# Delta rule: the next batch's key projections placed around the inverse's first levels

## The reference, cut to what matters

```python
q = _causal_dw_conv_silu(x @ Wq, conv_q)   # k and v likewise
q = _l2norm(q)
k = _l2norm(k)
def step(state, inp):
    q_t, k_t, v_t, a_t, b_t = inp
    retained = jnp.einsum('bhvk,bhk->bhv', state, k_t)
    rk = retained[..., None] * k_t[:, :, None, :]
    vk = v_t[..., None] * k_t[:, :, None, :]
    state = a4 * (state - b4 * rk) + b4 * vk
    o_t = jnp.einsum('bhvk,bhk->bhv', state, q_t)
    return (state, o_t)
```

## Time and profile before

| | us |
|---|---|
| median of 3 runs | 3834.85 |
| lowest and highest | 3829.89, 3841.63 |
| the profiled execution: its time | 3837.73 |
| its span | 3836.0 |
| PE busy | 3293.1 (86%) |
| DVE busy | 2394.9 (62%) |
| delta stage, first projection to last product | 1711.7 to about 3312 |

### The profile page before, as it was taken

The page is one execution under the profiler, slowest core; times in us unless marked ns, Lnnn a source line. Parts: engine busy times, 40 slices in busy tenths (PEclk is TensorE's granted clock), DMA queues, the critical chain, the costliest instruction groups (busy, mean ns, idle before and its releaser), DMA issues. The chain is left out here.

```text
span 3836.0 us, 48336 instructions
## 1 busy us (share of the span) xinstructions
PE 3293.1 (86%) x17898; PEld 2559.0 (67%) x17898; DVE 2394.9 (62%) x5793; ACT 1272.0 (33%) x2457; POOL 171.1 (4%) x165
## 2 busy tenths in 40 slices
PE   5999938889999999647989898989898989588887
PEld 2665524445999999625777777777777779455554
DVE  6788425544777777757676767575757574354542
ACT  2333202222444444314343434342434332023332
POOL 0000000024101111000000000000000000000000
PEclk8999958999999999867778787777768685588786
DMA  1000080022898899740101010101010100100000
GB/s 62 22 17 11 12 159 12 11 82 96 313 323 317 320 320 317 247 143 28 39 29 39 29 40 28 39 29 39 29 39 29 37 18 1 58 12 20 14 17 11
DMA packets 203644, 326.78 MB, mean 85 GB/s; under 512 B 37449, under 2 KB 157522, under 8 KB 202258
## 3 DMA queue, kind: packets, MB, share of 16 engines
q1 hardware_dynamic: 196930, 305.94, 24.1%
q0 software_dynamic: 6480, 17.77, 1.2%
HBM read 275.15 MB, written 48.50 MB: 84 GB/s over the span
## 5 line engine op out<-in xcount | busy, mean ns | idle before, releaser
L767 PE MATMUL ex_ps<-ex_xbT,ex_w 128*128 128x128 f32 x4544 | 530.6, 275 | 0.6 <-issue 0.5
L767 PEld LDWEIGHTS ex_ps<-ex_xbT,ex_w 128*128 128x128 f32 x4544 | 524.1, 192 | 4.7 <-issue 0.7
L1376 PE MATMUL de_ps<-de_hT,de_w 128*128 128x512 f32 x640 | 312.0, 642 | 19.2 <-DMA de_w<-in_w_kqv_dram 13.8
L896 ACT ACTIVATE ex_t<-ex_ps,ex_b 128x128 f32<-128x128 f32 x568 | 208.5, 367 | 335.3 <-PE ex_ps L767 303.5
L711 PE MATMUL ex_ps<-ex_xT,ex_w 128*128 128x512 f32 x512 | 230.4, 607 | 12.5 <-DVE ex_gl L1008 9.1
L1376 PEld LDWEIGHTS de_ps<-de_hT,de_w 128*128 128x128 f32 x640 | 128.5, 208 | 167.5 <-issue 158.9
L1008 DVE SCALAR_TENSOR_TENSOR ex_gl<-ex_ps,ex_b,ex_t 128x128 f32<-128x128 f32 (+1 forms) x316 | 123.5, 391 | 137.1 <-ACT ex_t L896 69.8
L711 PEld LDWEIGHTS ex_ps<-ex_xT,ex_w 128*128 128x128 f32 x512 | 97.9, 194 | 132.0 <-issue 115.2
L1748 DVE SCALAR_TENSOR_TENSOR de_ya<-de_kx,de_taps,de_ya 128x512 f32<-128x512 f32 x192 | 141.9, 750 | 50.7 <-ACT de_ya L1596 46.1
L1492 PE MATMUL de_ps<-de_vb,de_DG 128*128 128x64 f32 x512 | 113.2, 422 | 56.9 <-DVE de_o L1921 47.6
L1008 DVE SCALAR_TENSOR_TENSOR ex_gm<-ex_ps,ex_b,ex_t 128x128 f32<-128x128 f32 (+1 forms) x316 | 121.7, 385 | 47.7 <-ACT ex_t L869 41.9
(11 more groups left out here) (377 smaller groups left out, 6316.4 us busy)
## 6 DMA issues: line engine op xcount, KB each, us to landing
ex_w<-in_w_all_dram SPq DMA_DIRECT2D x144, 1024.0 KB, 6.2
ex_w<-in_w_all_dram SPq DMA_DIRECT2D x72, 512.0 KB, 8.7
de_w<-in_w_kqv_dram SPq DMA_DIRECT2D x80, 256.0 KB, 2.8
de_ab<-alpha_d SPq DMA_DIRECT2D x8, 2048.0 KB, 7.2
ex_xb<-ex_xs_d SPq DMA_DIRECT2D x71, 129.0 KB
ex_xs_d<-ex_blank SPq DMA_DIRECT2D x71, 128.5 KB, 8.4
ex_w<-ex_y_d SPq DMA_DIRECT2D x16, 512.0 KB, 6.1
mx_xin<-in_x_dram SPq DMA_DIRECT2D x8, 512.0 KB, 3.8
```

Source lines behind the costliest of these rows:

```text
L767: m = pe.matmul(ps[:, n % 4, x * BLK:(x + 1) * BLK], w[:, k, part * HID + c * P:part * HID + (c + 1) * P], xbT[sx][:, k, :], start=(k == 0 ...
L896: act.activation(t1[:, n % 2, 0:BLK], ps[:, n % 4, 0:BLK], ACT.Identity, bias=b13[s][:, 0, n:n + 1]).then_inc(t1_ready, 1)
L1376: m = pe.matmul(ps[:, n % 2, :], w[:, g % SLOTS, k, n % 2 * P:(n % 2 + 1) * P], hT[:, k, :], start=(k == 0), stop=(k == KT - 1))
```

## The change

The iteration that prepares batch b now also projects the keys of batch b + 1, and convolves five of them.

- PE: `invert` is split into helpers. Three next keys stand ahead of `y5(0)`, one after each pair of y5 and each pair of x5, the eighth after the tail. The wait for `outr` is now behind x5(0), x5(1). The four value transposes use banks 4 to 7 and wait for all of x6 and x11, and no longer for `vbr`. The norms read `vx` instead of `ya`.
- ACT: copies of the next keys among the spreading and the copies of the inverse; five steps of the next keys among the squares, which go to `vx` (four slots) instead of `ya`. `spread_blocks` is split in two.
- DVE: two convolutions after the first y5 pair, one after the first y6 pair, two after the second y5 pair, and seven after the second y6 pair, with the value scalings among them; conv(0) to conv(4) of the next batch stand around the PQ products; conv(5), conv(6) and conv(7) in the scan. `query_norm` comes after `out_a(3)`.
- SP: hT and the first weights of b + 1 are requested behind the last projection of b; the scan's scales behind the wait for `od`.

The core of the diff:

```diff
+            def keys_in(b):
+                if b:
+                    sp.wait_ge(s["pj"], b * PROJ)
+                sp.dma_start(hT[:, :, :], hT_d[b]).then_inc(s["hT_ld"], 16)
+                for g in range(SLOTS):
+                    weights(b, g, b == 0)
...
+                    for g in range(4 if pb is None else 5, GROUPS):
+                        weights(b, g, False)
+                    if b < BATCH - 1:
+                        keys_in(b + 1)
+                    load_scan_scales(b)
+                if pb is not None:
                     sp.wait_ge(s["oTp"], pb * VTL + VTL)
                     sp.dma_start(xin[:, :, :], x_in[pb].rearrange("(t p) d -> p t d", p=P)).then_inc(s["x_ld"], 16)
+                if b is not None and b < BATCH - 1:
+                    weights(b + 1, 3, False)
...
                 pe.wait_ge(s["ktr"], b * NC + NC)
+                for n in range(EARLY):
+                    next_key(b, n)
+                pe.wait_ge(s["xc"], b + 1)
+                y5(0), y5(1)
+                next_key(b, EARLY)
+                x5(0), x5(1)
+                next_key(b, EARLY + 1)
                 if pb is not None:
                     pe.wait_ge(s["outr"], pb + 1)
...
+                x11(0), x11(1), y6(0), y6(1), x6(0), x6(1)
+                y5(2), y5(3)
+                next_key(b, EARLY + 2)
+                x5(2), x5(3)
+                next_key(b, EARLY + 3)
+                x11(2), x11(3), y6(2), y6(3), x6(2), x6(3)
...
+                for n in range(EARLY + 4, V0):
+                    next_key(b, n)
...
+                    next_cp(0), next_cp(1)
+                    spread_left()
+                    next_cp(2)
+                    spread_diagonal()
+                    next_cp(3)
+                    x5(0), x5(1)
+                    next_cp(4)
+                    x11(0), x11(1)
+                    step(8, CONV - 1)
+                    step(9, CONV - 1)
+                    x6(0), x6(1)
+                    next_cp(5)
+                    step(10, CONV - 1)
+                    x5(2), x5(3)
+                    next_cp(6)
+                    x11(2), x11(3)
+                    step(11, CONV - 1)
+                    step(12, CONV - 1)
+                    x6(2), x6(3)
+                    for n in range(13, CONV):
                         step(n, CONV - 1)
...
+                    for hd in range(4):
                         square(hd)
+                    next_step(0), next_step(1)
+                    square(4), square(5)
+                    next_step(2)
+                    square(6), square(7)
+                    next_step(3)
+                    next_cp(7)
+                    next_step(4)
...
-                        query_norm()
-                        for n in range(6):
-                            conv(n)
                         dve.wait_ge(s["cl_ld"], 32 * pb + 32)
                         decay_u(0)
+                        conv(5)
+                        first_state()
                         conv(6)
-                        first_state()
-                        conv(7)
                         first_out()
...
                         new_state(1)
-                        decay(4, 5)
+                        conv(7)
                         out_b(1)
...
+                        query_norm()
+                        sum_squares(0), sum_squares(1)
                         decayed_gram(2)
...
+                    y5(0), y5(1)
+                    conv(8)
+                    conv(9)
+                    y6(0), y6(1)
+                    conv(10)
+                    y5(2), y5(3)
+                    conv(11)
+                    conv(12)
+                    y6(2), y6(3)
+                    conv(13)
+                    conv(14)
+                    values(0), values(1)
+                    conv(15)
+                    values(2), values(3)
+                    for n in range(16, CONV):
+                        conv(n)
...
+                    next_conv(0)
                     dve.tensor_copy(ae[:, :, :], ab[:, :, :].rearrange("p h (c t) -> p c h t", t=C)[:, :, :, C - 1]).then_inc(s["nqr"], 1)
                     for c in range(NC):
                         dve.wait_ge(s["gq"], b * NC + c + 1)
                         dve.tensor_tensor(PQ[:, c, :, :], wide(pair(c)), ab[:, :, c * C:(c + 1) * C], ALU.mult).then_inc(s["pq"], 1)
+                        next_conv(c + 1)
```

More of the change, by code:

```diff
@@ L1326, in load_scan_scales @@
             def load_scan_scales(pb):
+                if pb:
+                    sp.wait_ge(s["od"], pb * NC)
                 sp.dma_start(g2[:, :, :, :], bg_d[pb]).then_inc(s["cl_ld"], 16)
                 sp.dma_start(gend[:, :, :], gend_d[pb].unsqueeze(0).broadcast_to([P, H, NC])).then_inc(s["cl_ld"], 16)
+            def keys_in(b):
[4 more added lines that the diff above has]
+                    weights(b, g, b == 0)
             def body(pb, b):
-                first = pb is None
                 if b is not None:
[L1333 to L1339, removed]
+                    if pb is None:
+                        keys_in(0)
+                        weights(0, 3, True)
+                    else:
+                        weights(b, 4, False)
                         sp.wait_ge(s["pq"], pb * NC + NC)
@@ L1362, in _, with proj @@
             pe.wait_ge(s["folded"], 1)
-            def proj(b, n, first):
-                if n >= 2 or not first:
+            def proj(b, n):
+                if n >= 2 or b:
                     pe.wait_ge(s["cp"], b * PROJ + n - 1)
@@ L1482, in invert @@
                 if pb is not None:
                     pe.wait_ge(s["outr"], pb + 1)
[L1484 to L1521, removed]
@@ L1555, in body @@
                 else:
-                    for n in range(V0, Q0):
-                        proj(b, n, True)
+                    for n in range(K0, Q0):
+                        proj(b, n)
                     for c in range(NC):
@@ L1588, in cp, with tap, next_cp, next_step @@
                         act.activation(gate[:, n - G0, :], ps[:, n % 2, :], ACT.Silu).then_inc(s["cp"], 1)
[L1590 to L1591 removed]
+                def tap(n, b=b):
+                    if b * CONV + n >= 3:
                         act.wait_ge(s["act"], b * CONV + n - 2)
[L1593 to L1594 removed]
                     act.wait_ge(s["cp"], b * PROJ + n + 1)
[L1596 to L1598 removed]
+                    act.activation(ya[:, (b * CONV + n) % 3, :], xp(b, n)[:, 3:3 + SEQ], ACT.Copy, scale=taps[:, col_of(n), 3:4]).then_inc(s["tap"], 1)
+                def next_cp(n):
+                    if b < BATCH - 1:
+                        cp(n, b + 1)
+                def next_step(n):
+                    if b < BATCH - 1:
+                        step(n, 7, b + 1)
+                def silu(n, b=b):
                     act.wait_ge(s["cv"], b * CONV + n + 1)
[L1600 to L1603 removed]
+                    act.activation(xp(b, n)[:, 3:3 + SEQ], ya[:, (b * CONV + n) % 3, :], ACT.Silu).then_inc(s["act"], 1)
+                def step(n, last, b=b):
+                    silu(n, b)
                     if n + 2 <= last:
[L1605 removed]
+                        tap(n + 2, b)
+                    elif last == CONV - 1 and b < BATCH - 1:
+                        tap(n + 2 - CONV, b + 1)
                 def u(c):
```

135 lines of the change are left out of this document (82 added, 53 removed).

## The result

The changed kernel takes 3708.59 us in the median of four runs (3686.40 to 3721.58); the kernel before 3834.13 beside it. The ratio is 0.9665, 95% interval 0.9606 to 0.9723. The profiled execution took 3696.21 us (span 3694.4), 141.5 less than that of before.

A forecast was written before the change was run, and what follows sets the result against it. Bound: a chain of half-clock inverse (48 us), tail, keys, scan and DVE's work. Two periods of 158.3 and five of 177.5 make 1204 against 1346.9: -143, +15 for ends, -128; 3707 by the median, likeliest 3708, range 3615 to 3805.

The forecast's parts named there:

- the signs that the prediction had named as wrong: Clock 0.50 from y6 on, grams later than 55 us, or DVE idle while PE waits in the scan.
- Keys in the idle time: Three key projections, 5.2 us, fill PE's idle 6.7 us before the inverse; about 1 us idle, clock high, nothing saved directly.
- Inverse at the high clock: Inverse products take half their low-clock time, 11.7 us a pair instead of 23.4; x6 ends at 32, 16 us saved.
- the first rival: The clock falls inside the inverse: 9 us a period, 63 on top of the forecast, 3770, up to 3815; chance 0.26.
- DVE late next, PE idle for 15 us, the clock down for the grams: Before the grams: DVE's convolutions and ACT's last silu delay them to 50 instead of 55.7; PE idles from 35.
- Tail: Grams and norms: two of seven at the high clock, 15.7 us; period 158.3 with a high tail, 177.5 with a low.
- Scan: Key block of 13.8 us and 3.51 us wait gone; convolution 7 and query norm cost 0, at most 5.2 us.
- Ends: Batch 7's later convolutions cost +10 us, a clock fall before batch 0's inverse +5 us.
- The row of the select stage: Profile row: after short bursts with pauses of 0.96 and 0.52 us, the clock went from 1.00 to 0.51.
- the rule beside it: Short idles between groups of matmuls make the clock swing, so the inverse would not keep the high clock.

The follow-up runs named there:

- e4: The changed kernel with the three early next keys behind y5(1) instead of ahead of y5(0); 3798.66 us, ratio 0.9909 to the kernel before.
- e3: The changed kernel with next keys 3 to 7 spread among the inverse's narrow products, none behind the tail; 3737.05 us, ratio 0.9726 to the kernel before.
- e7: e6 with convolutions 11, 13 and 14 moved earlier on DVE, ACT's steps moved to fit, and eight unused matmuls; 3586.04 us, ratio 0.9356.
- e6: The changed kernel with the keys spread as in e3 and twelve timed unused matmuls ahead of the grams; 3631.70 us, ratio 0.9459.
- e2: The changed kernel with convolutions 13 to 19 of each batch made over 8 of 512 tokens, work left out; 3621.69 us, ratio 0.9441.
- e1: The changed kernel with ten unused 512-column matmuls behind the value transposes, in PE's idle time ahead of the grams; 3701.71 us, ratio 0.9636.

## Why the prediction was right

The total, 3708 against 3708.59, is closer than its steps, and that is luck. Two errors of some 60 us each cancelled, and the four runs lie up to 35 us apart; the profiled one took 3696.21 us where 3710 was forecast for it. Of the signs that the prediction had named as wrong, two came: a clock of 0.50 within the inverse (from x6 on, not from y6), and grams later than 55 us (58.8 to 64.6). No period was near 158 or 177.

- *Keys in the idle time.* Right in four of seven batches: 1.12 us idle, y5 pair in 3.79 us. In batches 0, 4 and 5 the clock fell within the y5 pair, which the forecast had for batch 0 alone; it made the grams 5.5, 3.0 and 2.8 us later. There was no delay of y5(0) by ACT, and by the weights in batch 0 alone (a DMA wait of 4.37 us). e4 prices the step at 10.6 us a period.
- *Inverse at the high clock.* This step failed, much as the first rival had it. In every full period the clock fell ahead of the second y5 pair: in four at 14.9 to 15.2 us, when x6 had just begun, in the other three at 15.8 to 18.9, in y6 or x6. x6(3) ended at 42.3 to 45.5 (48.1 in batch 0), not 32. The rival's 9 us a period is the measured size: the high-tail period is 167.1, against a forecast of 158.3, so +62 us over seven. In e3, e7 and most batches of e6 the second pair took the 3.79 us that the forecast assumed, with a wide product between y6 and x6.
- *DVE late next, PE idle for 15 us, the clock down for the grams.* Right in kind: 12.1 us idle, released by ACT's last silu, with DVE busy. The distance from the inverse's end to the grams, forecast 18, was 16.5. e2 confirms it, with ACT as the next limit close behind.
- *Tail.* Forecast two of seven high; five were. The price of a low one, forecast 19.2, was 15.0 and 15.7. In place of 5 x 19.2 = 96 us the two low tails cost 31; with the 11 us of the slow starts the odd periods cost 42: -54 us. I had set the chance of a rise by the three of eight before. Nothing I read could tell which batches would rise, so the count of five was outside what the working could give, and no run settles it.
- *Scan.* Right: `decay_u(0)` in time, 12.3 us between the first two u_products (forecast 12.4), and 77.9 us from there to the next inverse (before 78.3). Convolution 7 and the query norm cost nothing.
- *Ends.* Batch 0: +5.5 in its inverse, as forecast. Batch 7: grams at 62.4, +6.7 instead of +10, but its tail was high, where it had been low before. From the last `y5(0)` on the kernel took 7.7 us less.

The row of the select stage, and the rule beside it, pointed at the right danger. But by the Trainium skill ("TensorE: Matmul & The Clock Gate", section "A second HAM failure mode: psum-queue depth-cycling") it is short idles between groups that do it. For the fall that cost the most the trace does not bear that out: from y5(0) to the fall at 14.9 us PE waited once, for 0.23 us. The early falls of batches 0, 4 and 5 fit it better, with 1.12, 1.12 and 2.51 us of idle time just ahead of y5(0); but in batches 1 to 3 and 6 the same 1.1 us brought no such fall.

## What to carry to other kernels

Read the granted clock at the start, in the middle and at the end of a chain of small matmuls: moving useful work into the idle time ahead of it pays by its own length and by what follows. When a faster engine ends up waiting for another, look at whether that wait lowers its clock for the next group; where no real work fits, unused matmuls that end right at the release gave 67 us here, while the spread keys of e3 by themselves lost 28. Before a rearrangement is tried, such a filler is a cheap first experiment: in the kernel before it gave 96 us. And order the queue of the engine that is late next by what the waiting group needs: two convolutions moved into idle time gave 4.5 us a period.

## What was not expected of the hardware

- The clock fell with PE busy: in four batches it went from 1.00 to 0.50 between 5.5 and 5.8 us after x11 had begun, in products of 64 columns on 64 rows, with one wait of 0.23 us. In the kernel before it stayed at 0.50 through 48.0 us of inverse with PE busy 46.33. In the scan the same width on 128 rows, with wide projections and grams between, ran 32.1 us at 1.00. Width, rows, the transposes in x11 and the wide products between them were not told apart.
- The tail has two courses that the idle time ahead of it does not tell apart. In e1 the clock rose about 4 us into the grams behind 2.32 us, and was low for nearly the whole 26 us of the tail behind 3.63; in e2 it rose behind 6.0 us, and in the change behind 12.12 in one batch and not behind 12.11 in another. With PE busy 27.34 of 27.4 us, the low course kept 0.50 to its end.
- The same program differed from run to run by up to 35 us (3686 to 3722), and by 17 us with the filler (3632 to 3649). The number of low tails, at about 15 us each, is the likely source; only one execution of each kernel was profiled, so this is argued, not shown.
